# Loads in order of need, TensorE busy while tokens load, constants written later, the output in two steps: a one-core attention and expert layer

## The reference

```python
xn = _layernorm(x, axis=-1)
x = x + _L0_attn_ref(xn, wq, wk, wv, wo) + _L0_ffn_ref(xn, router_w, w1, w2, w3)
# attention: 16 query heads and 4 key/value heads of 16 channels, rotary, causal softmax, times wo
# experts: router scores of 8 experts, the best two, softmax of the two scores;
#          silu(x w1) * (x w3), times w2 in bfloat16, 64 hidden channels per expert, weighted sum
```

## Time and profile before

| | |
|---|---|
| median of 3 runs | 290.76 us (290.53 to 291.65) |
| the profiled execution, its own time | 290.62 us |
| its span in the trace | 288.9 us |
| instructions | 6905 |
| HBM read, written | 4.46 MB, 2.10 MB |

### The profile page before, as it was taken

How to read it: one execution, slowest core, us unless ns; L and a number is a source line. 1 busy time by engine, 2 the same in 40 slices (tenths; PEclk the granted TensorE clock), 3 DMA queues, 4 the chain that set the end, 5 groups by cost and what they waited for, 6 DMA issues and landing times.

```text
span 288.9 us, 6905 instructions
## 1 busy us (share of the span) xinstructions
PE 262.5 (91%) x2307; PEld 115.8 (40%) x2307; DVE 227.5 (79%) x312; ACT 244.4 (85%) x518; POOL 125.8 (44%) x260
## 2 busy tenths in 40 slices
PE   0868599999999999999999998999999999999996
PEld 0534355434344233334343443445523233433454
DVE  3663978999999999998999999995799898033342
ACT  1589876988999999999999998986689989898941
POOL 8386657363458418951135335246005414035020
PEclk9999889999999999999999999999999999999999
DMA  7537074110307103407371001023000300131307
GB/s 238 168 74 138 14 125 110 40 20 2 75 1 111 23 0 77 109 15 120 86 172 41 2 3 37 3 57 73 1 3 16 97 3 0 41 72 19 75 18 166
DMA packets 49106, 17.67 MB, mean 61 GB/s; under 512 B 43120, under 2 KB 48560, under 8 KB 49072
## 3 DMA queue, kind: packets, MB, share of 16 engines
q1 hardware_dynamic: 48384, 16.43, 26.8%
q10 hardware_dynamic: 688, 0.79, 0.8%
HBM read 4.46 MB, written 2.10 MB: 23 GB/s over the span
## 4 chain that ended last, share of the span: by engine, by line
PE 64%; DVE 12%; issue 8%; ACT 6%; POOL 5%; DMA 4%; POOLq 0%; SPq 0%; ACTq 0%
PE ps L808 18%; PE ps L790 13%; DVE PM L657 11%; PE ps L775 10%; PE ps L749 6%; PE ps L827 4%; ACT PR L543 3%; PE ps L848 3%; DMA HT<-HB 3%; PE ps L817 2%; PE ps L767 2%; PE ps L846 2%; PE ps L739 2%; DMA STACKS<-MIXED 1%; PE ps L835 1%
## 5 line engine op out<-in xcount | busy, mean ns | idle before, releaser
L543 ACT ACTIVATE PR<-ps,SCALE 128x512 f32<-128x512 f32 (+1 forms) x320 | 182.5, 654 | 15.7 <-PE ps L790 13.5
L657 DVE TENSOR_REDUCE PM<-ps 128x8 f32<-128x1024 f32 x144 | 167.8, 1218 | 9.0 <-PE ps L775 7.7
L453 POOL TENSOR_SCALAR_AFFINE_SELECT PR<-PR 128x512 f32<-128x512 f32 x64 | 39.8, 635 | 94.7 <-ACT PR L543 94.7
L808 PE MATMUL ps<-PR,VA 128*32 128x512 f32 (+3 forms) x768 | 78.1, 495 | 0.5 <-ACT OA L550 0.5
L790 PE MATMUL ps<-STACKS 64*128 64x512 f16 (+3 forms) x384 | 75.2, 327 | 2.9 <-ACT PR L543 1.4
L775 PE MATMUL ps<-STACKS 64*128 64x128 f16 (+2 forms) x640 | 59.2, 263 | 5.4 <-DVE PM L657 3.7
L790 PEld LDWEIGHTS ps<-STACKS 64*128 64x128 f16 x384 | 24.3, 93 | 57.0 <-ACT PR L543 43.6
L775 PEld LDWEIGHTS ps<-STACKS 64*128 64x128 f16 x640 | 27.1, 95 | 36.7 <-issue 32.1
L468 POOL TENSOR_TENSOR HB<-MIXED,GATE 128x512 bf16<-128x512 f32 x16 | 16.5, 1043 | 30.0 <-DVE MIXED L711 29.6
L808 PEld LDWEIGHTS ps<-PR,VA 128*32 128x32 f32 x768 | 17.0, 108 | 25.9 <-issue 21.1
L749 PE MATMUL ps<-WP,XT 128*128 128x392 f32 x64 | 25.7, 536 | 1.6 <-ACT XT L489 1.6
(11 more groups left out here) (92 smaller groups left out, 234.0 us busy)
## 6 DMA issues: line engine op xcount, KB each, us to landing
X<-x SPq DMA_DIRECT2D x8, 256.0 KB, 6.3
out<-X SPq DMA_DIRECT2D x16, 128.0 KB, 1.9
MIXED<-w SPq DMA_DIRECT2D x3, 512.0 KB, 3.8
STACKS<-MT SPq DMA_DIRECT2D x64, 2.0 KB
WP<-w_proj ACTq DMA_DIRECT2D x1, 392.0 KB, 4.3
WO<-wo ACTq DMA_DIRECT2D x1, 256.0 KB, 6.2
STACKS<-MIXED SPq DMA_TRANSPOSE x16, 3.6
MT<-MPW SPq DMA_TRANSPOSE x16, 2.5
```

The lines of the kernel that those rows point to most:

```text
L453: mask = g.affine_select(out=blk, in_=blk, compare_op=ALU.is_ge, fill=0.0, base=0, pattern=[[0, GRP], [1, P]], channel_multiplier=-1)
L543: a.activation(PR[:, k % RING, j, 0:width], bank(step)[:, 0:width], ACT.Exp, scale=SCALE[:]).then_inc(s_exp, 1)
L657: v_.tensor_reduce(spots, two_banks(step).rearrange("p h (a s n) -> p h a s n", a=2, n=P), AX.X, ALU.max).then_inc(m_max, 1)
L808: mm = t_.matmul(o_bank[VW * j:VW * (j + 1), CHUNK - width:CHUNK], VA[:, b * KVH + grp, kb, :], PR[:, n % RING, j, at:at + width], start=i ...
```

## The change

- **Loads.** SP issues two token loads (four tiles), waits for `WP`, then issues the other six, then the load of `WO`, which ACT no longer issues; the mask copy follows.
- **TensorE at the start.** After the identity is there, PE makes `WARMING` = 9 transposes of the identity into the product bank, which nothing reads, and then enters its order.
- **Constants.** `MPW`, `TS`, `PM`, `VA` and `RANK` are written in a new step `F` of POOL, which stands after the first two `n` of its order.
- **Orders.** All five orders are written anew. On DVE `W` now stands ahead of the first `z`; on PE the `p` stands ahead of the first `x`, the first two projections stand ahead of the third transpose, and projections 2 and 3 behind transposes 2, 3 and 4. PE has 15 `m`, 5 `J` and 7 `x` between its first `m` and its first `s`, where it had 17, 6 and 7.
- **Output.** `y` is split: `Y` (share) does the four matmuls with `W2` and takes the bank; `y` does those with `WO` later in the same bank. The slot of `HT` is free after `Y`, and `HELD` is 6.

The diff follows, the long order strings cut to their first and last lines.

```diff
--- before.py
+++ after.py
@@ -19,6 +19,9 @@
 TOKENS = BATCH * SEQ
 TILES = TOKENS // P
 LOADS = TILES // 2
+
+FIRST_LOADS = 2
+WARMING = 9
 HD = 16
 QH, KVH = 16, 4
 GRP = QH // KVH
@@ -43,7 +46,7 @@
 SLABS = QH + KVH * PILE
 VW = 32
 RING = 3
-HELD = 4
+HELD = 6
 LN_EPS = 1e-5
 BIG = 1e30
 
@@ -111,35 +114,35 @@
 
 ORDER = dict(
     PE=(
-        "xpxxPjjjxxxjxxjjjjmmmmmxxxmmJmJmmJmxmxxmJmJxmmJmsxmJmssmssmssmssmsvssmssmvssmsvmssmJmsmssvsmsssmvmss"
...
-        "vssyasseessvssEEssvsaevsssyssyssrrssvssvssveavEEryaaayayyy"),
+        "pxxPjjxxxjjxxxjjjjmmmmmmxxxmJmmJxmJmmxJmxmJmxsmssmssmssmssmJmssmsvmxssmvssmsmsvsmssmJmssmsvsmsmssvms"
...
+        "aaEssYrssysseessvssYYassyvssvssEvssyssEEssvssvssEessYavvyaYrryYaaYyyYaaYyy"),
     ACT=(
-        "xNxNxzzjllxxNNzzljjlxxNxjjNjNjjNllzzzxxzzxllJzzJJxxxJJlzxJlsxJssssssssssssssssssvJssssssssssvsssssss"
...
-        "ssvassssesessssassesssssssssssevaaaaa"),
+        "xxNNzxllxjxjjzzzxljlNxjjxNNNjjNNllzzzxzxxJllxzJzxJzxJzJxssssssssslJlsssxsssssssssvJsssssssssssvsslJs"
...
+        "sssssssvasseessssssssssssssssaevaaaaa"),
     DVE=(
-        "nnzWzzpnPjjznjjjjjjmmmmmMmmmmmmmMmmmmMmmmmmMmmmmmmmmmmmmmMmmmmmmmrrbbrbmmmmmmmMmmmmmmmmmmmmmMmmmmmmm"
...
-        "mmmmmmmmmeMEEeemmmEEemmrbmmmymmmmMyyEeEyeeEEyeyrrbbeEErbyyyyy"),
+        "nnWzzpnPzjjznjjjjjjmmmmmmmMmmmMmmmmmmmmmmMMmmmmmmmmmmmmmmMmmmmmmmmrbmmmmrrbbmMmmmmmmmmmmmmmmmmmmMmmm"
...
+        "mmmmmmmMEeeeEmyEmrebmymmmmmEmmmmMEyyeerEbyyeeyEEEeEyrrbbyyyyy"),
     POOL=(
-        "nnnjjllnjjlljjRlljjMllqqMMlsssMqssssMsssssllqsssMlqssMslqqlqlssMslsMssMMMcccssssssMEsssssEEsEEMsssss"
-        "EMsEEEEsssMEEsssEEEE"),
+        "nnFnjjllnjjlljjRlljjMlMlqsqMMsslqlssssqMslssssslMssqqllqqssMssMMsllssssMMcccsssMMsssEEssssssEsEEMsss"
+        "sEEMssssMEEEEsssEEEEE"),
     SP=(
-        "kkkkkktkkututtuutkukktutkukktkkuctcctuuttuuwtuwwyytwwuwtwwyyutuywwwwwwyyywwyyyyyyyy"),
+        "kkkkkktukktuttkuutkkutkukktutkkuttcccutuuttuuwwwwtwutuwwyytwuywwwyywwyywwwyyyyyyyyy"),
 )
-KINDS = dict(W="largest", p="range", P="scales", n="moments", N="spread", R="deviations", z="norm", x="turned", j="project", J="projected", q="rotated", l="parts", k="stacks", m="maxima", M="rows",
+KINDS = dict(F="frames", W="largest", p="range", P="scales", n="moments", N="spread", R="deviations", z="norm", x="turned", j="project", J="projected", q="rotated", l="parts", k="stacks", m="maxima", M="rows",
              t="rows_turned", u="rows_placed", s="scores", v="product", r="untwisted", b="quotients", g="rank", G="weigh", c="cast", e="experts",
-             E="factors", w="hidden", a="flat", y="output")
+             E="factors", w="hidden", a="flat", Y="share", y="output")
 
 BANKS_V, BANKS_S = 4, 3
-FILLED_V = dict(project=1, maxima=2, untwisted=1, experts=1, factors=1, output=1)
+FILLED_V = dict(project=1, maxima=2, untwisted=1, experts=1, factors=1, share=1)
 FILLED_S = dict(turned=1, projected=1, scores=1, flat=1)
 
 
...
@@ -290,7 +293,7 @@
 
 
         READ_OUT = dict(turned=xb_sb, project=v_taken, projected=v_spread, maxima=m_max, scores=s_exp, untwisted=o_norm,
-                        experts=silu, factors=hidden, flat=a_sb, output=y_ready)
+                        experts=silu, factors=hidden, flat=a_sb, share=y_ready)
 
         def bank_free(step, at=0):
             before = places[step][at][1]
@@ -304,9 +307,12 @@
         @block.sync
         def _(sp):
             for n in range(LOADS):
+                if n == FIRST_LOADS:
+                    sp.wait_ge(w_in, 16)
                 sp.dma_start(X[:, 2 * n:2 * n + 2, :], x[2 * n * P:(2 * n + 2) * P, :].rearrange("(s p) d -> p s d", p=P)
                              ).then_inc(x_in[n], 16)
 
+            sp.dma_start(WO[:], wo.rearrange("(k p) n -> p k n", p=P)).then_inc(wo_in, 16)
             sp.wait_ge(ruled, 7)
             sp.dma_start(MASKS[ROWS:P], MASKS[0:ROWS]).then_inc(halved, 16)
 
@@ -323,7 +329,7 @@
                 elif kind == "hidden":
                     sp.wait_ge(gated, n + 1)
 
-                    after(sp, y_ps, n - HELD + 1)
+                    after(sp, y_half, n - HELD + 1)
                     sp.dma_start_transpose(HT[:, n % HELD], HB[:, n % 2]).then_inc(h_turned[n % 2], 16)
                 elif kind == "rows_placed":
                     b, c, grp = JOBS[n]
@@ -355,9 +361,8 @@
 
             g.memset(IDF[:], 0.0).then_inc(zeroed, 1)
             g.memset(MASKS[:], 0.0).then_inc(zeroed, 1)
-            g.memset(MPW[:], 0.0).then_inc(zeroed, 1)
             g.memset(NHALF[:], -0.5).then_inc(zeroed, 1)
-            pool.wait_ge(zeroed, 4)
+            pool.wait_ge(zeroed, 3)
             g.affine_select(out=IDF[:], in_=IDF[:], compare_op=ALU.not_equal, fill=1.0, base=0,
                             pattern=[[-1, P]], channel_multiplier=1).then_inc(made, 1)
             upper, last = slice(0, ROWS), ROWS - 2
@@ -370,16 +375,18 @@
                 g.affine_select(out=t[upper], in_=t[upper], compare_op=ALU.is_ge, fill=fill, base=last,
                                 pattern=[[0, t.shape[1]]], channel_multiplier=-1).then_inc(ruled, 1)
             g.memset(ONE[:], 1.0).then_inc(made, 1)
-            g.memset(TS[:, :, 0:QH, 3, :], 0.0).then_inc(framed, 1)
-            g.memset(TS[:, :, QH:SLABS, 3, 2:HD], 0.0).then_inc(framed, 1)
-            g.memset(TS[:, :, QH:SLABS, 3, 0:2], -1.0).then_inc(framed, 1)
-            g.memset(PM[:], -BIG).then_inc(framed, 1)
-            g.memset(VA[:, :, :, HD:VW], 1.0).then_inc(made, 1)
-            for e in range(E):
-                g.memset(RANK[:, e:e + 1], float(E - e)).then_inc(made, 1)
 
             for kind, n in steps_of("POOL"):
-                if kind == "moments":
+                if kind == "frames":
+                    g.memset(TS[:, :, 0:QH, 3, :], 0.0).then_inc(framed, 1)
+                    g.memset(TS[:, :, QH:SLABS, 3, 2:HD], 0.0).then_inc(framed, 1)
+                    g.memset(TS[:, :, QH:SLABS, 3, 0:2], -1.0).then_inc(framed, 1)
+                    g.memset(PM[:], -BIG).then_inc(framed, 1)
+                    g.memset(MPW[:], 0.0).then_inc(zeroed, 1)
+                    g.memset(VA[:, :, :, HD:VW], 1.0).then_inc(made, 1)
+                    for e in range(E):
+                        g.memset(RANK[:, e:e + 1], float(E - e)).then_inc(made, 1)
+                elif kind == "moments":
                     pool.wait_ge(ve, n + 1)
                     two = slice(2 * n, 2 * n + 2)
                     g.tensor_tensor(RSTD[:, two], VE[:, two], NHALF[:, two], ALU.pow).then_inc(rstd, 1)
@@ -432,6 +439,8 @@
                 elif kind == "rows":
 
                     pool.wait_ge(m_row, n + 1)
+                    if n == 0:
+                        pool.wait_ge(zeroed, 4)
 
                     after(pool, m_turned[n % 2], 16 * (n // 2))
                     rows = MX[:, n % 2].rearrange("p i a h -> p i h a")
@@ -473,7 +482,6 @@
             a = nc.scalar
             act.dma_start(WP[:], w_proj.rearrange("(k p) n -> p k n", p=P)).then_inc(w_in, 16)
             act.dma_start(CS[:], tables).then_inc(tab_in, 16)
-            act.dma_start(WO[:], wo.rearrange("(k p) n -> p k n", p=P)).then_inc(wo_in, 16)
 
             for kind, n in steps_of("ACT"):
                 step = (kind, n)
@@ -712,13 +720,16 @@
                 elif kind == "output":
 
                     dve.wait_ge(y_ps, n + 1)
-                    v_.tensor_tensor(X[:, n, :], bank(step)[:, 0:D], X[:, n, :], ALU.add).then_inc(y_ready, 1)
+                    v_.tensor_tensor(X[:, n, :], bank(("share", n))[:, 0:D], X[:, n, :], ALU.add).then_inc(y_ready, 1)
 
         @block.tensor
         def _(pe):
             t_ = nc.tensor
 
             pe.wait_ge(made, 1)
+
+            for _ in range(WARMING):
+                t_.transpose(o_bank[:, 2 * P:3 * P], IDF[:], IDF[:])
 
             for kind, n in steps_of("PE"):
                 step = (kind, n)
@@ -834,18 +845,24 @@
                     for k in range(KT):
                         mm = t_.transpose(bank(step)[:, k * P:(k + 1) * P], AO[:, n, k * P:(k + 1) * P], IDF[:])
                     mm.then_inc(a_ps, 1)
-                elif kind == "output":
+                elif kind == "share":
                     if n == 0:
                         pe.wait_ge(w_cast, 3)
-                        pe.wait_ge(wo_in, 16)
 
                     bank_free(step)
-                    pe.wait_ge(a_sb, n + 1)
                     pe.wait_ge(h_turned[n % 2], 16 * (n // 2 + 1))
                     for k in range(EF // P):
-                        t_.matmul(bank(step)[:, 0:D], HT[:, n % HELD, k, :], W2[:, k, :], start=(k == 0), stop=False)
+                        mm = t_.matmul(bank(step)[:, 0:D], HT[:, n % HELD, k, :], W2[:, k, :], start=(k == 0), stop=False,
+                                       skip_group_check=True)
+                    mm.then_inc(y_half, 1)
+                elif kind == "output":
+                    if n == 0:
+                        pe.wait_ge(wo_in, 16)
+
+                    pe.wait_ge(a_sb, n + 1)
```

(38 more changed lines are left out.)

8 lines of the change are left out of this document (removed).

## The result

Six runs of the changed kernel had a median of 293.92 us (293.01 to 294.34); six of the kernel before, beside them, 291.15 us (290.76 without the one at 468.88). The ratio is 1.0086, with a 95% interval of 1.0065 to 1.0106: 1.9 to 3.1 us slower. Three runs far above the others of their kernel are left out of the ratios: one here of the kernel before, at 468.88 us, and two of the twelve of `c_warm28` (experiment 5), at 294.5 and 294.6 us. The profiled execution took 293.01 us.

What follows compares the result with a forecast made beforehand. It saw DVE, ACT and PE nearly full from 60 to 180 us, then PE alone; start -0.35, middle -0.7 and tail -0.6 made -1.65 us from 290.62, 288.97; it said 289.0, range 286.8 to 291.2.

Steps and rivals of the forecast that it cites:

- part 3: PE's clock in the first two projections: a somewhat earlier rise, gain 0.35 us, between a 1.4 gain and a 0.9 loss.
- part 6: First maxima to first score: fewer `m` and `J`, ACT's exponentials earlier; -0.7 us taken, bounds 0 and -2.9.
- part 1: Constants moved to step F at the start: first tile gains nothing; GpSimd's writes beside DVE cost 0.3 us on the path.
- Rival C: At the start, GpSimd's constant writes block VectorE, up to 3 us ahead of the first rotary step; 292.2 us, chance 0.12.
- sum at the first maxima: All terms of the start up to the first row maxima: -0.35 us, with bounds -1.6 and +1.5.
- start of the projections: Fewer PE steps before the first projection: it begins at about 10.2 us, 0.6 us gained.
- part 4: Order behind the first two projections: the third stands behind x2, x3 and x4; 0.6 us loss, between 0 and 1.1.
- Part 7: Split output: no price for bank or score waits; fewer PE stalls in the tail, -0.6 us, bounds 0 and -1.
- Part 5: Token loads held behind `WP` on SP at the start: price 0, bounds -0.3 and +0.5 us.

Runs made afterwards that it cites:

- c_warm28: The changed kernel with 28 transposes of the identity at the start instead of 9; 290.96 us, ratio 1.0006 to the kernel before.
- a_const: The changed kernel with all constants, MPW too, written ahead of POOL's order again; 292.33 us, ratio 1.0062 to the kernel before.
- f_keptconst: `a_kept` with all constants also written ahead of POOL's order; 290.17 us, ratio 0.9964 to the kernel before.
- b_kept: The kernel before with groups of 4 unread transposes added in PE's order around the first `m`; 290.08 us, ratio 0.9969 to the kernel before.
- e_all: The changed kernel with 28 transposes at the start, added groups at the first maxima and constants ahead of POOL's order; 287.75 us, ratio 0.9892 to the kernel before.
- c_fivem: The changed kernel with five `m` instead of six ahead of transposes x8 to x10 on PE; 292.76 us, ratio 1.0066 to the kernel before.
- g_warmkept: `b_kept` with MPW written ahead of VA and 26 transposes at the start; 289.91 us, ratio 0.9945 to the kernel before.
- a_kept: The changed kernel with groups of 4 unread transposes added in PE's order around the first `m`; 291.41 us, ratio 1.0018 to the kernel before.

## Why the prediction was wrong

It forecast 289.0 us and said 0.12 for slower; measured was 293.92, 2.5 us over the kernel before by the ratio.

- **The step that failed is part 3: the clock was priced only for the first two projections.** The stretch of the first maxima, on which part 6 builds, was given no clock term at all. The earlier trace rows showed a lower stretch at the first maxima, with work stacked up behind it, and I used it only as evidence on the transposes of the start. No term and no rival asked what an order that leaves PE sparse for longer does to it. It went from 3.4 to 6.8 us or more, and keeping PE busy there gave back 2.0 us, 0.9 of which the kernel before can gain too.
- **The second step that failed is part 1's price of GpSimd's writes.** I took 0.3 us on the path; the two `z` alone lost 0.8, and without the writes the time fell by 0.7 us (`a_const`) and, with the clock out of the way, by 1.6 (`f_keptconst`), both uncertain by 0.8. The block was the right reading of 1.06 against 0.17 us in the earlier trace rows. The Trainium skill, "SBUF — State Buffer", section "Who interferes with whom", has the same; the traces agree, with VE at 0.71 us beside VA's write and ending with it (11.64 and 11.61 us). Rival C's mechanism was thus real and in its place. Its price of 2 us was too high for the first maxima, which were 0.8 us late in all; for the whole time 1.6 us comes near it.
- **The sum at the first maxima** was -0.35 us with bounds -1.6 to +1.5; it was +0.8. The start of the projections was taken at -0.6 and was +0.25 (11.02 instead of 10.2); the clock of the first two at -0.35 and was +0.35 (4.71 against 4.36); for part 4 +0.6 was taken and +0.2 is left.
- **The nine transposes** did nothing that could be measured. They took 2.18 us, not the 3.0 that 0.33 each gave, and the rest behind them was 4.2 us, not 3.2. Part 3 doubted them because of this rest, but still took the gain of 0.35. That 28 would help, the text did not see.
- **Part 4's price was not too low.** Its third projection ended near 19.1 (its rotary step at 19.16) instead of 18.1. But this was 3.4 us behind the end of the second tile's, where I had 3.9: the lateness came in ahead of it.
- **Part 6 was wrong in both halves.** The first `s` was at 52.29 instead of 49, since the clock ate what the moved `m` and `J` gave: in `f_keptconst`, with clock and constants out of the way, it was at 48.88. And an earlier start gave the middle nothing: that first `s` is 2.6 us ahead of `b_kept`'s 51.44, and the two times are level. `e_all` had its first `m` at 27.86, its first `s` at 47.64, and PE was busy for 112.96 of 120 us from 60 to 180, not more.
- **Part 7 was right in its waits:** none of PE behind `Y`, none for HT at the end. -0.6 was taken; joining the steps cost 0.8 us, give or take as much. That the `WO` matmuls would take 0.7 us longer it did not see.
- **Part 5:** no cost shows in the profile, and the third load was there when VectorE came to it at 9.95; the timing has 1.2 us that go with the clock of the runs, for which it had no term.

Taken together, the clock at the first maxima (1.1 us over the kernel before, uncertain by 1) and the constants (0.7 to 1.6) are together about as large as the loss of 2.5 us, and with both gone the changed kernel is level with `b_kept`.

What makes the new orders stretch the lower level stays open. It isn't the sixth `m`. One candidate has some support: four of ACT's `N` stand later, so `z` 8 begins at 35.83 instead of 33.73, and PE's dense work with it at 36.0 instead of 34.5. In `c_fivem` PE did wait for this `z`. An order with the `N` where they were wasn't tried.

## What to carry to other kernels

Where TensorE becomes sparse for some us and dense work follows, price the clock of that work at both levels, and see whether a reordering makes the sparse stretch longer; a few transposes that nothing reads are a cheap test. Transposes ahead of the first data should last nearly until the data are there: here nine with 4.2 us of rest behind them gave nothing, 28 with 1.1 us gave 2.3. Writes of constants on GpSimd are not free beside VectorE's tensor_scalar steps (1.63 us instead of 0.72 for two here); place them where no such step is due. Ahead of POOL's order they still held the first VE (1.07 us in `a_const`, 0.17 in the changed kernel). Compare orders only at the same mean granted clock: `g_warmkept`'s twelve runs span 3 us, and stand exactly in the order of their clocks.

## What the runs showed of the hardware

The granted clock in the trace is 1.00 in the first 15 us of the changed kernel, although the projections there take 0.65 us for an instruction and 0.37 later; only matmul durations show the lower level at the start. Later the column does show it, and in `g_warmkept`, where 26 transposes came first, it shows it in the first 15 us too (0.50 from 10 to 12 us). Transposes alone brought the upper level (28 in 5.15 us, then projections at 2.90 us for eight) and, 24 of them between the first `m`, kept it there in `a_kept`. The lower level in the column lasted about 0, 3.4, 6.8 or 10.2 us in the profiles other than `g_warmkept`'s, and its length differed between runs of one kernel. In the kernel before, 25 runs of a session at a mean granted clock of 0.994 had a median of 290.70 us, and four at 0.981 one of 291.68.
